# Rebuilding a two-layer RWKV and expert kernel: tokens put into expert slots in DRAM, the last group split, and the key-value products on GpSimd

## The reference, cut to what matters

```python
# layer 0, attention: a scan over time, per channel
ww = u + kt; p = maximum(pp, ww); e1 = exp(pp - p); e2 = exp(ww - p)
y = (e1 * aa + e2 * vt) / (e1 * bb + e2)
ww2 = pp + w; p2 = maximum(ww2, kt); e1 = exp(ww2 - p2); e2 = exp(kt - p2)
aa, bb, pp = e1 * aa + e2 * vt, e1 * bb + e2, p2        # then sigmoid(r) * y @ W_out
# layer 1, attention: five inputs mixed from x and the token before it, then
kv = k_t[..., :, None] * v_t[..., None, :]              # 16 heads of 8 x 8
y = einsum('bhk,bhkj->bhj', r_t, S + u[None, :, :, None] * kv)
S = d_t[..., None] * S + kv                             # then a norm per head, * silu(g), @ Wo
# experts: 8 of them, the top 2 per token, hidden width 512
h = act(xf @ W1[e]); out += gates[:, e:e+1] * (h @ W2[e])   # gelu with biases in layer 0, silu in layer 1
```

## Time and profile before

| | |
|---|---|
| three timed runs | 666.99, 672.38, 674.42 us; median 672.38 |
| profiled execution, first to last instruction | 673.3 us |
| mean granted TensorE clock | 0.838 of full |
| busy share of the span | PE 76%, PE weight load 55%, DVE 49%, ACT 30%, POOL 38% |
| DMA | 70.27 MB, mean 104 GB/s |

### The profile page before, as it was taken

One profiled execution on the slowest core, in us unless ns is written; L12 is line 12 of the kernel. 1 busy time (PEld: TensorE's weight loads), 2 busy tenths in 40 slices (PEclk: granted clock), 3 DMA queues, 4 the chain that ended last, 5 costly groups with the idle time before them and its releaser, 6 DMA issues. The chain is left out here.

```text
span 673.3 us, 7874 instructions
## 1 busy us (share of the span) xinstructions
PE 514.8 (76%) x2600; PEld 371.7 (55%) x2600; DVE 330.1 (49%) x624; ACT 203.3 (30%) x457; POOL 256.1 (38%) x238
## 2 busy tenths in 40 slices
PE   6952444787988789997788679997788996777763
PEld 5420224476977677346355544534454986767663
DVE  2799997533600015435986687534777546100000
ACT  2042510325535335345122013025111443033330
POOL 1062600762465643102644000306975223646440
PEclk9785665696998899976999777568989998689897
DMA  7000005255564655203100201402342543757623
GB/s 234 0 0 1 0 28 190 52 133 145 178 203 136 220 200 154 65 28 88 47 8 2 62 0 57 182 12 67 84 100 82 173 143 85 242 161 216 185 86 125
DMA packets 28744, 70.27 MB, mean 104 GB/s; under 512 B 5938, under 2 KB 10662, under 8 KB 28704
## 3 DMA queue, kind: packets, MB, share of 16 engines
q1 hardware_dynamic: 18656, 57.43, 27.1%
q0 software_dynamic: 5888, 10.25, 6.2%
q10 hardware_dynamic: 4160, 2.10, 1.1%
HBM read 62.40 MB, written 9.18 MB: 106 GB/s over the span
## 5 line engine op out<-in xcount | busy, mean ns | idle before, releaser
L437 POOL DMA_INDIRECT y_rows<-ys,dest x92 | 98.1, 1067 | 171.2 <-ACT ys L600 156.0
L430 POOL DMA_INDIRECT xg<-h_rows,source x92 | 93.0, 1010 | 152.2 <-DVE source L1266 108.3
L839 PE MATMUL PP<-w_ring,hid 128*128 128x128 f32 x736 | 109.3, 296 | 29.9 <-ACT hid L587 15.0
L839 PEld LDWEIGHTS PP<-w_ring,hid 128*128 128x128 f32 x736 | 95.4, 201 | 44.5 <-issue 22.9
L824 PE MATMUL PP<-xs,w_ring 128*128 128x128 f32 x736 | 100.3, 289 | 1.5 <-ACT xs L574 0.8
L824 PEld LDWEIGHTS PP<-xs,w_ring 128*128 128x128 f32 x736 | 96.3, 206 | 6.6 <-issue 5.7
L1275 DVE SCALAR_TENSOR_TENSOR x<-PP,gate,x 128x512 f32<-128x512 f32 x8 | 6.0, 750 | 163.6 <-PE PP L885 94.9
L600 ACT ACTIVATE ys<-PP,slot_gate 128x128 f32<-128x128 f32 x92 | 33.8, 370 | 128.7 <-PE PP L839 101.3
L587 ACT ACTIVATE hid<-PP,b1q 128x128 f32<-128x128 f32 x184 | 51.9, 379 | 52.1 <-PE PP L824 36.1
L463 POOL TENSOR_TENSOR arena<-arena 128x512 f32<-128x512 f32 x32 | 38.0, 1189 | 21.7 <-DVE arena L1322 19.4
L945 PE MATMUL PP<-arena,consts 128*128 128x512 f32 x64 | 35.5, 637 | 11.0 <-POOL arena L463 10.7
(11 more groups left out here) (193 smaller groups left out, 747.7 us busy)
## 6 DMA issues: line engine op xcount, KB each, us to landing
w_ring<-experts_dram SPq DMA_DIRECT2D x92, 512.0 KB
h_rows<-htok ACTq DMA_DIRECT2D x4, 512.0 KB
xg<-h_rows,source POOLq DMA_INDIRECT x92
y_rows<-ys,dest POOLq DMA_INDIRECT x92
x<-x_t_dram SPq DMA_DIRECT2D x4, 256.0 KB, 5.9
out_t_dram<-x SPq DMA_DIRECT2D x4, 256.0 KB, 3.7
H<-wmod_dram SPq DMA_DIRECT2D x1, 768.0 KB, 6.7
consts<-consts_dram SPq DMA_DIRECT2D x1, 704.0 KB, 7.5
```

Source lines behind the costliest of these rows:

```text
L430: pool.indirect_dma_start(xg[:, n % XG, :], None, h_rows[h], bass.IndirectOffsetOnAxis(source[:, h % 2, q:q + 1], 0)).then_inc(s_xg[n % XG ...
L437: pool.indirect_dma_start(y_rows[h], bass.IndirectOffsetOnAxis(dest[:, h % 2, q:q + 1], 0), ys[:, n % YR, :], None, bounds_check=TOPK * T ...
L839: last = pe.matmul(ps, hid[:, n % HID, c * P:(c + 1) * P], w_ring[:, n % WR, FH + c * P:FH + (c + 1) * P], start=(c == 0 and h >= NB), sto ...
```

## The change

Nearly every function is written anew; the computation is the same. The parts are:

1. **Expert rows.** Tokens are put into their slots in DRAM (`puts`, one indirect write per 128 tokens and choice), so no inverse is made. Slots are read four blocks at a time and results stored by plain DMAs on SyncE's queue, and `gets` fetches each token's two rows by indirect reads. The gate is applied when a token's rows are summed, by a product with a diagonal (`dg`). The slots are filled with zeros at the start.
2. **Groups.** (1, 1) is split: its two blocks of 512 tokens are two groups of 15 expert blocks. There are 5 groups with 23, 23, 23, 15, 15 = 99 blocks. Weight buffers go from 6 to 5.
3. **Routing** has no softmax: the gates come from a tanh of the difference of two logits.
4. **First attention**: clamped differences and sigmoids on ScalarE; no elementwise work on GpSimd.
5. **Second attention**: v goes to DRAM and comes back spread, by DMA, into four buffers; GpSimd multiplies k into them in place; VectorE scans and multiplies by r. Batch 0 works on 1024 tokens at once (8 steps), batch 1 on 512 (8 steps for its first block, then 8 for its second).
6. **Layer norms**: the centring matrix is one product, ScalarE takes square and copy from PSUM, the spreading is four 128-column products.
7. **Orders** of all five queues are new.

```diff
-NQ = (TOPK * T + NE * (P - 1)) // P
-XG, WR, YR, HID = 8, 6, 4, 2
+GROUPS = ((0, 0, (0, 1)), (0, 1, (0, 1)), (1, 0, (0, 1)), (1, 1, (0,)), (1, 1, (1,)))
+NQ = [(TOPK * P * t + NE * (P - 1)) // P for t in GT]
+WR, XG, HID, YR, VS = 5, 3, 2, 6, 4
...
     "POOL":
-        "a4 b4 g15 s2 g5 s g s g2 s6 g s g3 s g s2 g3 s g s2 g2 s g2 s g s2 g3 s g s2 g2 s g s g s2 g s11 a4 "
...
+        "p32 g16 k8 g16 p16 k16 p8 g6 p8 g26",
...
+            def puts():
+                for g in range(NG):
+                    for t in range(GT[g]):
+                        for k in range(TOPK):
+                            yield
...
+                            pool.indirect_dma_start(xg_rows[g], bass.IndirectOffsetOnAxis(row_of[:, g, k, t:t + 1], 0),
+                                                    htok[:, t, :], None, bounds_check=NQ[g] * P - 1,
+                                                    oob_is_err=False).then_inc(s_put, 16)
+            def gets():
...
+                            if t == 0 and k == 0:
+                                for p in range(YR):
+                                    pool.wait_ge(s_yst[p], 16 * ((Q0[g + 1] - 1 - p) // YR + 1))
...
+                            pool.indirect_dma_start(yt[:, k, t, :], None, y_rows[g],
+                                                    bass.IndirectOffsetOnAxis(row_of[:, g, k, t:t + 1], 0)).then_inc(s_got[t // TPB], 16)
+            def products():
...
+                            pool.tensor_tensor(vs[m % VS][:, 0:width], A["K"][:, at0:at0 + width], vs[m % VS][:, 0:width],
+                                               ALU.mult).then_inc(s_kv[b], 1)
...
+            def slots():
+                        if u == 0:
+                            sp.wait_ge(s_put, 16 * TOPK * G0[g + 1])
...
+            def rows():
+                        sp.wait_ge(s_ys, n + 1)
+                        sp.dma_start(y_rows[g][q * P:(q + 1) * P, :], ys[:, n % YR, :]).then_inc(s_yst[n % YR], 16)
...
             def attn0_exponents(b):
...
-                dve.scalar_tensor_tensor(A["p"], A["K"], col(C_U0), prev, ALU.add, ALU.max).then_inc(s_arg[b], 1)
-                dve.wait_ge(s_arg[b], 2)
-                dve.scalar_tensor_tensor(A["d2"], A["K"], col(C_U0), A["p"], ALU.add, ALU.subtract).then_inc(s_arg[b], 1)
+                dve.tensor_tensor_scan(A["pp"][:, 1:T + 1], wneg.broadcast_to([P, T]), k, NEG_BIG,
+                                       ALU.add, ALU.max).then_inc(s_pp[b], 1)
+                dve.wait_ge(s_pp[b], 1)
+                dve.tensor_tensor(A["D"], k, A["pp"][:, 0:T], ALU.subtract).then_inc(s_dl[b], 1)
...
+            def attn1_state(b, part):
+                    dve.wait_ge(s_kv[b], n + 1)
+                    link(dve.tensor_tensor_scan(S[:, 1:width + 1], A["dec"][:, span], vs[m % VS][:, 0:width], start, ALU.mult, ALU.add))
...
+                    link_prod(b, j, n, part, dve.tensor_tensor(prod[n % 2][:, 0:width], A["R"][:, span], S[:, 0:width], ALU.mult))
```

More of the change, by code:

```diff
@@ L349, in _, with step, loads_before, in_unit @@
+        def step(b, i, j):
+            return j if b == 0 else HK * i + j
+        def loads_before(b, n):
+            return n if b == 0 else HK + n
+        def in_unit(g, u):
+            return range(UNIT * u, min(UNIT * (u + 1), NQ[g]))
         @block.sync
         def _(sp):
+            for i in range(BPB):
+                sp.dma_start(x_blk(0, i), blk(x_d, i)).then_inc(s_x[0][i], 16)
+                if i == 0:
+                    sp.dma_start(ident[:], const_d[:, 17, :]).then_inc(s_ident, 16)
@@ L405, in _, with results @@
+            def results():
+                for b in range(NB):
+                    for i in range(BPB):
+                        yield
+                        sp.wait_ge(s_xup[b][i], 4)
+                        sp.dma_start(blk(out_d, BPB * b + i), x_blk(b, i)).then_inc(s_done, 16)
+            merged(ORDER.get("SP", ""), w=weights(), l=slots(), y=rows(), v=spreads(), o=results())
             sp.wait_ge(s_done, 16 * NBLK)
@@ L496, in _ @@
+            merged(ORDER.get("POOL", ""), p=puts(), g=gets(), k=products())
         @block.scalar
@@ L498, in _, with table @@
             loaded = [None]
-            def table(*sets):
+            def table(sets):
                 if loaded[0] not in sets:
@@ new lines, in attn0 @@
+                table(SIGMOID)
+                act.wait_ge(s_kvr[b], 3)
+                act.activation(A["R"], pair(KVR_PAIR[b][2]), ACT.Sigmoid).then_inc(s_r0[b], 1)
+                yield
+                act.wait_ge(s_den[b], 1)
+                table(LOG)
+                act.activation(A["E2"], A["D"], ACT.Ln, bias=ones[:, 0:1]).then_inc(s_ln0[b], 1)
+                yield
+                table(EXP)
+                act.wait_ge(s_ln0[b], 1)
+                act.activation(A["E2"], A["E2"], ACT.Exp, scale=-1.0).then_inc(s_rden[b], 1)
@@ new lines, in second, with tail @@
+            def second():
+                yield from layer_norm(0, 1, (0, 1))
+                yield from attn0(1)
+                yield from layer_norm(1, 1, (0, 1))
+                yield from route(1)
+                yield from layer_norm(2, 1, (0, 1))
+                yield from attn1_proj(1)
+            def tail(i):
+                yield from group_norm(1, (i,))
+                yield from layer_norm(3, 1, (i,))
+                yield from route(3 + i)
+            merged(ORDER.get("ACT", ""), a=first(), b=second(), c=tail(0), d=tail(1), t=turned(), h=hidden(), w=copied())
@@ new lines, in attn1_sums @@
+            def attn1_sums(b, part):
+                for j in range(HK):
+                    n = step(b, part[0], j)
+                    yield
+                    pe.wait_ge(s_prod[b], n + 1)
+                    if j == 0:
+                        pe.wait_ge(s_y0[b], BPB)
+                    for k, i in enumerate(part):
+                        last = pe.matmul(sums(b, i), headsum[:, j, :], blk(prod[n % 2], k), start=(j == 0), stop=(j == HK - 1),
+                                         skip_group_check=True)
+                    last.then_inc(s_yps[b], 1)
@@ new lines, in second @@
+            def second():
+                yield from layer_norm(0, 1, (0, 1))
+                yield from attn0(1)
+                yield from attn0_out(1)
+                yield from layer_norm(1, 1, (0, 1))
+                yield from route(1)
+                yield from finish(1)
+                yield from layer_norm(2, 1, (0, 1))
+                yield from attn1_proj(1)
+                yield from attn1_bonus(1)
+                yield from attn1_sums(1, (0,))
+                yield from attn1_sums(1, (1,))
@@ L1011, in _, with tail @@
+            def tail(i):
+                yield from group_norm(1, (i,))
+                yield from layer_norm(3, 1, (i,))
+                yield from route(3 + i)
+                yield from finish(3 + i)
+            merged(ORDER.get("PE", ""), m=modulation(), a=first(), b=second(), c=tail(0), d=tail(1), t=turned(), f=all_first(), s=all_second())
         @block.vector
@@ L1424, with tail @@
+            def tail(i):
+                yield from group_norm(1, (i,))
+                yield from layer_norm(3, 1, (i,))
+                yield from route(3 + i)
+                yield from finish(3 + i)
+            merged(ORDER.get("DVE", ""), m=modulation(), k=constants(), a=first(), b=second(), c=tail(0), d=tail(1))
 def kernel(**inputs):
```

1692 lines of the change are left out of this document (814 added, 878 removed), and 29 rows, old and new, of the table ORDER.

## The result

The changed kernel took **644.3 us** (642.6 to 650.3 over 4 runs) where the kernel before took 670.3 (667.0 to 674.4): a ratio of 0.970, 95% interval 0.961 to 0.979. It is faster by 26 us; the forecast was 570. The profiled execution took 644.2.

What follows compares the result with a forecast made beforehand. No engine is full over the whole, so the time was taken as a chain of stages: 110 + 88 + 53 + 42 + 20 + 14 + 53 + 86 + 0 + 83 + 21 = 570 us, against a 673.3 us span; range 530 to 625.

Steps and rivals of the forecast that it cites:

- Group 1 and its rows: Stage of group 1's expert blocks, then its gets and sums: 88 us, before 124; 23 blocks at 2.6 us make 60.
- Groups 4 and 5: Last two groups' expert blocks: 83 us, before 67; 30 blocks at 2.6 us make 78, plus 5 for sums.
- groups 3 to 5: Group 3 with the states of batch 1, 86 us, and groups 4 and 5, 83 us: together 169 us.
- head norm: Stage after the state of batch 0: 20 us as before, with batch 1's gets covered, 7 us to spare.
- To the first block: Start until the first expert block: 110 us, before 124.6; set by VectorE, slots known near 82, 16 puts costing 20.
- Group 1's blocks: Expert blocks of group 1 at 2.6 us each, bounds 2.2 and 2.92, with TensorE's floor at 2.2.
- rival B: Expert blocks: 512-byte rows move as fast as weights, 53 blocks are 0.4 us quicker, 21 less, 549 us; chance 0.12.
- State of batch 0: Eight scan steps of the second attention: 42 us, before 61, with four collisions with GpSimd products at 2.4 us each.
- Rival A: VectorE and GpSimd's shared port: products block VectorE, indirect DMAs slow near scans, group 3 stays at 100; 599 us; chance 0.20.
- Two layer norms: Stage between head norm and the projections of batch 1: 14 us, before 17.
- projections: Projections of batch 1 until layer 1's first block: 53 us, before 60, with the clock left at 0.65.
- The idle 23 us: Wait of the last group for routing and inversion, 563 to 586 us before: 0, as puts finish during group 3's blocks.

Runs made afterwards that it cites:

- e14: Changed kernel with plain DMAs to and from fixed rows in place of indirect puts and gets, where the kernel before took 670.9: 567.6 us, 0.850 of it.
- e1: Changed kernel with plain DMAs of the same bytes, still issued by GpSimd, in place of indirect puts and gets; the kernel before took 644.2: 569.5 us.
- e12: Changed kernel itself, nothing edited, on a chip free of late handoffs: 571.8 us (568.8 to 581.6), 0.885 of the kernel before.
- e4: Changed kernel with the 24 key-value products made by VectorE in place instead of GpSimd: 581.5 us.
- e3: Changed kernel with 32 one-column matmuls added on TensorE at about 50 us, to shift its instruction loads: 575.1 us.
- the probe: Changed kernel plus phases of 16 timed handoffs beside GpSimd's DMAs, where the kernel before took 670.9: up to 5.64 us in place of 2.76.
- e9: Changed kernel with six phases of 16 TensorE-to-ScalarE handoffs added behind it, GpSimd's DMAs varied, on a chip without late handoffs: 2.76 us each.

## Why the prediction was wrong, step by step

**The step that failed** is the price of the puts and gets in *Group 1 and its rows* and in *Groups 4 and 5*. The 16 gets of group 1 were "2.5 for the last row store, 20 for the issues, 2.1 to land, 3 for the last sums", 28 us; they measured 51 (from the last row copy at 185.9 to 237). The puts and gets that run beside blocks had no price at all: a block was 2.6 us with or without them, and in groups 4 and 5 it took 3.6. All were counted by GpSimd's own time and the landing, as if TensorE and ScalarE worked on beside them. On the chip of the record every long train beside short products holds TensorE's results back from their readers. Group 1 and its rows took 119 us instead of 88, groups 3 to 5 took 196 instead of 169, the head norm 28 instead of 20. The same kernel without late handoffs took 87, 164 and 23, and 571.8 in all. The sum had no term for it; its last sentence had only named the case, "something that shows in neither TensorE's nor the DMA engines' share", and guessed at SyncE.

It could have been read. The waits of the kernel before (above) hold 37 us of ScalarE and 11 of VectorE ended by an unnamed releaser, beside or just behind trains of 3 to 12 indirect DMAs. I gave the 4.3 us a block of that stretch no cause, and put what the last group's blocks take above 2.2 us down to gathered rows and row buffers, though the chain there has three unknown pieces of 11.9 us (it can be followed back to 367 us only). Between the two kinds of chip lie 27 us for the kernel before (671 against 644) and 73 for the changed one (645 against 572). That the indirect trains make the 73 is shown by e14, whose chain has no unknown piece; that they make the 27 is inferred, no edit of the kernel before was run. The changed kernel has fewer indirect DMAs, 128 instead of 184, but in trains of mostly 16 that nothing interrupts. From the rows of before alone 73 could not have been worked out; but the term would have been in the sum, and the range would have reached further up.

*To the first block*: 118 against 110. VectorE was as quick as priced (first put at 84.0 against 82), but four of the first five puts ran beside its elementwise instructions and took 1.61 to 3.08 us, the longest beside the VectorE instruction shown:

```profile
89.57 1.77 POOL L491 DMA_INDIRECT xg_rows<-htok,row_of  x1 [0.30 <-issue]
91.59 2.28 DVE L1278 TENSOR_TENSOR dg<-ident,gates_sb 128x2048 f32<-128x2048 f32 x1
91.64 3.08 POOL L491 DMA_INDIRECT xg_rows<-htok,row_of  x1 [0.30 <-issue]
95.03 0.97 POOL L491 DMA_INDIRECT xg_rows<-htok,row_of  x1 [0.31 <-issue]
```

The 16 took 25 us, not 20; the earlier trace rows had shown it. The Trainium skill, SBUF — State Buffer, "Who interferes with whom", infers that descriptor generation is not held up by VectorE's `tensor_tensor`. The prediction took its 1.93 us to speak against that, and 3.08 against 0.97 looks the same. But e1 agrees with the page: its 16 plain puts ran beside four of the same VectorE instructions (among them a `tensor_tensor` of 1.44 us at 88.00; that of 2.28 us starts as the puts end) and took 8.64 us, against 8.55 and 8.58 in the quiet probes. Only the indirect form was held up. It also reads its row numbers from SBUF; that this read is what waits is a guess.

*Group 1's blocks*: 2.6 us was too much. Without late handoffs its 23 blocks leave 2.09 us apart (first row copy at 124.3, last at 170.2 us in e12), at 297 GB/s: rows of 512 bytes move nearly as fast as weights, which is rival B's mechanism. The Trainium skill, DMA: Bandwidth & Descriptors, "Specifications", puts line rate at 512 bytes, and this agrees. TensorE is busy for 44.5 of the 46 us from 124 to 170 at a granted clock of 1.00, about 2.0 us a block, so the "floor" of 2.2, read at 0.95, was too high as well. In the record the blocks left 2.85 us apart. What B gains there, the rows give back: 36 us from the last block to the second sum against 28 (seven until the stores have landed, sums in TensorE's written order). That e12's stage came to 87 us for the forecast 88 is luck: the blocks 14 us cheaper, the rows 8 dearer, and 5 until the first row copy that were not priced. In groups 4 and 5 a block with the sums between took 2.7 us in e12 (29 intervals in 79.5 us), near the forecast, and 3.6 in the record (104.9).

*State of batch 0*: 38 against 42, right in kind. Three scans ran beside a product of GpSimd and cost 1.68 more each, and one product on VectorE (2.84 for 1.23) 1.61 more, 6.7 in all, not four at 2.4:

```profile
301.62 3.97 DVE L1350 TENSOR_TENSOR_SCAN arena<-arena 128x1024 f32<-128x1024 f32 x1
305.63 2.84 DVE L1359 TENSOR_TENSOR arena<-arena 128x1024 f32<-128x1024 f32 x1
```

Rival A's price is therefore small; GpSimd's products are worth 6 us where no handoff is late (e4 against e3, which has the small matmuls; the unedited kernel did not run on that chip), and nothing that could be measured where some are.

*Two layer norms* 18 against 14, *projections* 52 against 53 with clock 0.74, *end* 21 against 21. *The idle 23 us* are gone in e12, as forecast.

The range (530 to 625) held the time of one kind of chip and not that of the other. Faster was right on both. That 571.8 lies so near the forecast 570 owes something to errors that cancel, as in group 1's stage.

## What to carry to other kernels

In a trace, add up what the waits put down to "remote" or an unknown queue before pricing anything, and see what else runs beside them; a term with no name is still a term. Long unbroken trains of indirect DMAs beside TensorE's chains of short products are a risk that a second chip may show and the first not: with plain DMAs, whose trains are also shorter, the time was the same on both, and trains of four had nearly none. And run the unedited kernel in each set: three edits seemed to give 63 to 75 us here and one 28; beside the unedited 571.8 us none of them gains more than 3, and the drains cost 44.

## What the hardware showed that was not expected

- Where the kernel before takes 671 us, TensorE's results reach ScalarE and VectorE late beside trains of indirect DMAs: handoffs take up to 5.64 us in place of 2.76 in the probe, and in the kernel ScalarE reads at 171.0 us what TensorE's records have started by 159. It begins 3 to 14 us (in the kernel) or 12 to 15 us (in the probe) after the start of a train and ends at most 3 us after the train. It was seen beside the indirect form and many short products alone; none of 32 handoffs from VectorE and none of 16 from one wide product was late. Whether it is the chip or a state of it isn't known, nor what lies behind it; the loads of TensorE's instructions do not set the places.
- The idle time costs clock as well: from 154 to 172 us of the record TensorE is busy for 4.5 of 18 us, and from 172 to 198 us it is granted 0.70 (e12 had 1.00 from 124 to 170). Over the whole of group 1's stage it is 0.84 against 0.93.
- An indirect DMA of 64 KB takes GpSimd 0.94 to 0.97 us and 0.30 of pause while VectorE is quiet, and up to 3.08 beside VectorE's instructions; of the plain ones in e9's probe, 16 took 8.6 us in all.
